# Layer 1 written out batch by batch, with the routing of layer 1's experts spread through it

## What is computed

```python
h    = layernorm(x)                      # rows of 256
g    = h @ Wr.T                          # 8 logits a row
top2 = the two largest of g, softmax over these two
y    = sum over the two experts e of  p_e * (silu(h @ Win[e].T) @ Wout[e].T)
x    = x + tanh(gate) * y
```

## Time and profile before

| | us |
|---|---|
| median of 3 runs (1465.41 to 1466.18) | 1465.86 |
| the profiled execution, its own time | 1465.79 |
| its span, first to last instruction | 1464.1 |
| PE busy (8832 matmuls) | 1292.1 (88%) |
| DVE busy | 1042.8 (71%) |
| ACT busy | 920.9 (63%) |
| POOL busy | 754.2 (52%) |

### The profile page before, as it was taken

One profiled execution on the slowest core, in us unless ns is written; L12 is line 12 of the kernel. 1 busy time (PEld: TensorE's weight loads), 2 busy tenths in 40 slices (PEclk: granted clock), 3 DMA queues, 4 the chain that ended last, 5 costly groups with the idle time before them and its releaser, 6 DMA issues. The chain is left out here.

```text
span 1464.1 us, 29786 instructions
## 1 busy us (share of the span) xinstructions
PE 1292.1 (88%) x8832; PEld 949.8 (65%) x8847; DVE 1042.8 (71%) x2336; ACT 920.9 (63%) x3577; POOL 754.2 (52%) x1068
## 2 busy tenths in 40 slices
PE   3899999999963899999999999999999994359991
PEld 2234444444432688888888888888888883349991
DVE  6466666666544888888888888888888877835554
ACT  1245454554534988888888888888888863313230
POOL 2355464645432566666666666666655542723331
PEclk8799999999985999999999999999999996569996
DMA  6443333323002311011110111101120005422225
GB/s 128 110 78 54 71 57 65 68 54 70 15 1 79 113 37 37 0 36 36 36 36 0 36 36 36 36 0 36 38 70 1 2 1 176 138 77 80 90 73 172
DMA packets 134339, 83.50 MB, mean 57 GB/s; under 512 B 67309, under 2 KB 129774, under 8 KB 134256
## 3 DMA queue, kind: packets, MB, share of 16 engines
q1 hardware_dynamic: 125280, 72.50, 19.4%
q0 software_dynamic: 3744, 8.43, 1.6%
q10 hardware_dynamic: 5232, 1.54, 0.5%
HBM read 50.01 MB, written 34.00 MB: 57 GB/s over the span
## 5 line engine op out<-in xcount | busy, mean ns | idle before, releaser
L1358 POOL TENSOR_TENSOR head_rstd<-head_rstd,minus_half 128x4 f32<-128x4 f32 x192 | 240.8, 1254 | 15.0
L1348 ACT ACTIVATE squares<-ps 128x128 bf16<-128x128 f32 x768 | 202.1, 282 | 49.9 <-PE ps L1320 39.7
L1320 PE MATMUL ps<-l_wb,xq 128*128 128x512 f16 (+1 forms) x1024 | 211.3, 329 | 6.7 <-DVE xq L1282 4.6
L1428 POOL TENSOR_TENSOR prob<-prob,rinv 128x512 f32<-128x512 f32 x128 | 135.5, 1058 | 118.0 <-DVE rinv L1423 116.5
L1415 ACT ACTIVATE prob<-ps,nmax 128x128 f32<-128x128 f32 x512 | 182.7, 384 | 11.4 <-DVE nmax L1408 11.4
L1378 ACT ACTIVATE headsT<-ps,l_hln 128x256 f32<-128x256 f32 (+1 forms) x256 | 166.6, 678 | 25.6 <-PE ps L1371 25.6
L1348 ACT ACTIVATION_READ_ACCUMULATOR squares<-ps 128x1 f32 x768 | 163.5, 214 | 0.0
L1364 DVE TENSOR_TENSOR heads_n<-ps,head_rstd 128x512 f32<-128x512 f32 x192 | 131.5, 685 | 38.8 <-POOL head_rstd L1358 38.8
L656 DVE TENSOR_REDUCE nmax<-ps 128x4 f32<-128x512 f32 x128 | 85.1, 682 | 75.4 <-PE ps L649 75.2
L1320 PEld LDWEIGHTS ps<-l_wb,xq 128*128 (+1 forms) x1024 | 101.0, 99 | 53.6 <-DVE xq L1282 5.0
L1401 PE MATMUL ps<-headsT 128*128 128x128 f32 x1024 | 135.2, 275 | 0.3 <-issue 0.3
(11 more groups left out here) (303 smaller groups left out, 2762.6 us busy)
## 6 DMA issues: line engine op xcount, KB each, us to landing
slots<-blank_slot SPq DMA_DIRECT2D x16, 1161.0 KB, 5.6
taken<-slots SPq DMA_DIRECT2D x23, 258.0 KB, 2.8
w_out_raw<-in_wprojT SPq DMA_DIRECT2D x8, 512.0 KB, 4.4
raw<-in_winT SPq DMA_DIRECT2D x4, 1024.0 KB, 9.2
raw<-in_woutT SPq DMA_DIRECT2D x4, 1024.0 KB, 6.1
back<-picked SPq DMA_DIRECT2D x8, 512.0 KB, 7.2
q_stack<-q_parts SPq DMA_DIRECT2D x48, 64.0 KB
k_blocks<-k_parts SPq DMA_DIRECT2D x192, 16.0 KB
```

The costliest lines, as they stand in the source:

```text
L1320: last = e.matmul(out, xq[:, k, which, slot_at], weights(k, hl, c0, n), start=(k == 0 and hl == 0), stop=(k == KD - 1 and hl == 1))
L1348: last = e.activation(squares[:, 4 * n + h, :], A[n][:, h * HD1:(h + 1) * HD1], ACT.Square, scale=HD1**-0.5, accum_out=hss[:, 4 * n + h:4 ...
L1358: e.tensor_tensor(hr[:, four], hr[:, four], t["half"][:, four], ALU.pow).then_inc(g_r[n].sem, 1)
L1428: e.tensor_tensor(prob[:, kind, :, :], prob[:, kind, :, :], spread(rinv[:, kind, :], P), ALU.mult).then_inc(g_p[kind].sem, 1)
```

## The change

1. All 16 batches of layer 1 are written out; there is no loop. The order strings get new words, and every step of the routing becomes a piece of them: `GS`, `GR`, `GN` (statistics, 1/sqrt, normalised rows), `GT` (two transposes into `S[0]`), `GU` and `GH` (ScalarE's copy of the turned rows, and of the high half), `GO` (number and low half of the packet), `GL` (two matmuls for the logits into `S[0]`), `GX` (copy of the logits), `GC:0` to `GC:2` (the choice for four batches, 16 chained instructions in three parts), `GK` (ranks, into `S[0]`), `GA` (addresses, 8 instructions), `GZ:0` to `GZ:3` (two scattering DMAs each). A batch's steps follow its attention by one to four batches.
2. `SC:0` waits in round 2 for `GU`, in round 3 for `GX`, and after a group also for the first instruction of `GA`.
3. The input weights of the experts go into `wb`, whose raw half takes the loads; they start when the last projection (`A`) is done, 4 of 8 pieces are split in the attention's block, 4 after it. SP waits for all scattered packets at the block's end.
4. WP_RING is 2 instead of 4. The blank table is written in the first four batches, 4 DMAs in each.
5. The block behind holds only the count, the table of tiles, and the splitting of the last 4 pieces. `back`, for the last sum, lies in `wb`.

```diff
-WP_RING = 4
+WP_RING = 2
 ORDER1 = {
-    "tensor": "A:0+ TQ:1 SC:0 PV:0- SC:1 O-- TQ:2+ PV:1- A:1+ PT:0 TQ:0+ A:2++ RT@0++ A:3 PT:1",
+    "tensor": "A:0+ TQ:1 SC:0 PV:0- SC:1 O-- TQ:2+ PV:1- A:1+ PT:0 TQ:0+ A:2++ RT@0++ GT@1-- GK@2--- GL@2-- A:3 PT:1",
-    "vector": "PT:1- SC:0 N:2+ RN@3+++ SC:1 RQ:4@2+ RS@3++++ RQ:3@1+ RQ:0@0+ R:0 RQ:1@0+ O-- QM:0- N:0+ R:1 QM:1- "
-              "PT:0 Q:0- Q:1- Q:2- N:1+ Q:3- Q:4- RQ:2@0+",
+    "vector": "PT:1- GX@3-- GA@3--- SC:0 N:2+ RN@3+++ GN@0-- SC:1 RQ:4@2+ RS@3++++ RQ:3@1+ RQ:0@0+ R:0 RQ:1@0+ O-- QM:0- N:0+ "
+              "R:1 QM:1- GS@2- GO@2-- PT:0 Q:0- Q:1- Q:2- N:1+ Q:3- Q:4- RQ:2@0+ GC:0@3-- GC:1@0--- GC:2@1---",
-    "scalar": "RA:0@0+ TQ:0 ST:2+ RE@1++ RA:3@3++ VE- RA:1@2++ RA:2@1++ TQ:1 ST:0+ SC:0 SC:1 CH@0+ TQ:2+ ST:1+",
+    "scalar": "RA:0@0+ TQ:0 ST:2+ RE@1++ GU@2-- RA:3@3++ VE- RA:1@2++ RA:2@1++ GH@1-- TQ:1 ST:0+ SC:0 SC:1 CH@0+ TQ:2+ ST:1+",
-    "gpsimd": "RS@2++++ R:1+ SU:1++ CO@3++ SU:2+++ SU:0+++ R:0++",
+    "gpsimd": "RS@2++++ R:1+ SU:1++ CO@3++ SU:2+++ SU:0+++ R:0++ GR@1- GZ:0@2--- GZ:1@3--- GZ:2@0---- GZ:3@1----",
-    "sync": "CL@0+ BL@1",
+    "sync": "CL@0+ BL:0@0 BL:1@1 BL:2@2 BL:3@3",
 }
...
+            if j == 2 and b >= 2:
+                e.wait_ge(a_gu.sem, a_gu.at(b - 2))
+            if j == 3 and b >= 2:
+                e.wait_ge(v_gx.sem, v_gx.at(b - 2))
+            if j == 3 and b >= 3 and (b - 3) % GROUP == GROUP - 1:
+                e.wait_ge(v_pos.sem, v_pos.at((b - 3) // GROUP))
...
+    EXPERTS_AFTER = {
+        "scalar": (("VE", LAST, B - 1, J - 1), ("GU", B - 2, J * B + 2), ("GU", B - 1, J * B + J + 2), ("GU", B - 1, J * B + J + 2)),
+        "vector": (("GS", B - 1, J * B + 2), ("GN", B - 1, J * B + J), ("GO", B - 1, J * B + J + 2), ("GC", B - 1, J * B + 2 * J + 1, 2)),
+    }
...
+    @s.piece("GX", "vector")
+    def _(e, b, i):
+        e.wait_ge(pe_gl.sem, pe_gl.at(b))
+        e.tensor_copy(logit[:, b % GROUP, :], S[0][:, 0:NE]).then_inc(v_gx.sem, 1)
...
+    @s.piece("GZ", "gpsimd")
+    def _(e, b, i, q):
+        if b % GROUP != GROUP - 1:
+            return
+        g, one = b // GROUP, b - GROUP + 1 + q
...
+        for which in range(2):
+            e.indirect_dma_start(
+                out=t["slots"][:, :], out_offset=bass.IndirectOffsetOnAxis(ap=at_u[:, g % 2, which, q:q + 1], axis=0),
+                in_=packet[:, one % PACKETS, :], in_offset=None, bounds_check=NE * SHELF - 1,
+                oob_is_err=False).then_inc(sent[g % 2], 16)
...
-        "sync": (("CL", 0, -4),) * 4 + (("CL", 1, 0),) * 4,
+        "sync": (("CL", 0, -4),) * 2 + (("CL", 1, 0),) * 6,
...
     with nc.Block() as block:
-        s.run(block, starting,
-              lambda owner, b: rounds(ORDER1[owner], b, False), lambda owner: part(owner, B - AHEAD, B + 1), (1, B - AHEAD))
+        s.run(block, starting, None, lambda owner: [], (0, 0))
```

More of the change, by code:

```diff
@@ new lines, in layer1_attention @@
+    wr, m_stats, m_mv, m_rstd, m_rows, u, packet = (t[n] for n in ("wr", "m_stats", "m_mv", "m_rstd", "m_rows", "u", "packet"))
+    logit, same, hide, number, first, second = (t[n] for n in ("logit", "same", "hide", "number", "first", "second"))
+    most, place, picks, before, tally, shelf = (t[n] for n in ("most", "place", "picks", "before", "tally", "shelf"))
+    pos, at, at_u, lower, all_b = (t[n] for n in ("pos", "at", "at_u", "lower", "all_b"))
+    wr_in, sets = nc.alloc_semaphore("wr_in"), nc.alloc_semaphore("route_sets")
@@ new lines, in _ @@
+    @s.piece("GK", "tensor")
+    def _(e, b, i):
+        if b % GROUP != GROUP - 1:
+            return
+        g = b // GROUP
+        e.wait_ge(v_pick.sem, v_pick.at(g))
+        e.wait_ge(v_PT[0].sem, v_PT[0].at(min(i, LAST)))
+        if b + 1 < B:
+            e.wait_ge(a_gu.sem, a_gu.at(b + 1))
+        e.wait_ge(v_gx.sem, v_gx.at(b))
+        here = S[0][:, 2 * GE:3 * GE]
+        e.matmul(here, lower[:, :], picks[:, :, :], start=True, stop=False)
+        e.matmul(here, all_b[:, :], tiled(before[:, :], GROUP), start=False, stop=False)
+        for j in range(GROUP - 1):
+            last = e.matmul(S[0][:, 2 * GE + (j + 1) * NE:3 * GE], all_b[:, :], tiled(picks[:, j, :], GROUP - 1 - j),
+                            start=False, stop=(j == GROUP - 2))
+        last.then_inc(pe_gk.sem, 1)
@@ L1737, in _ @@
-            e.wait_ge(s_makes, 6)
-            turn(0)
-            for g in range(NG):
-                route(g)
-                if g + 1 < NG:
-                    turn(g + 1)
-                rank(g)
-            e.wait_ge(s_count, 1)
-            e.matmul(bank[4][:, 0:NE], all_b[:, :], before[:, NG, :], start=True, stop=True).then_inc(s_count, 1)
+            e.matmul(bank[4][:, 0:NE], all_b[:, :], before[:, :], start=True, stop=True).then_inc(s_count, 1)
         @block.vector
         def _(e):
-            chain = Chain(nc, "c_route", 21 * NG + 13)
+            chain = Chain(nc, "c_route", 17)
```

435 lines of the change are left out of this document (235 added, 200 removed).

## The result

| | before | after |
|---|---|---|
| median, us (4 runs each, on one chip) | 1465.63 (1464.25 to 1466.18) | 1490.76 (1490.30 to 1492.20) |
| ratio, 95% interval | | 1.0175 [1.0157, 1.0192] |
| span of the profiled execution | 1464.1 | 1489.1 |
| first update of x in layer 1 | 506.04 | 522.99 |
| last update of x | 1216.15 | 1273.15 |

The change makes the kernel 25.1 us slower. The three stretches give the whole of it: the first update of x comes 17.0 us later, the 64 rounds from the first update to the last take 750.16 us instead of 710.11 (40.1 more), and from the end of the last update to the experts' first matmul it is 1324.60 - 1273.63 = 51.0 us instead of 82.0 (31.1 less). What follows is 0.9 us shorter. 17.0 + 40.1 - 31.1 - 0.9 = 25.1 us, the 25.0 of the spans.

What follows compares the result with a forecast made beforehand. TensorE, busy 100 of every 100 us, was taken to bound layer 1's attention. The terms -31.5 + 6.8 + 17 + 8 + 18 + 16 = +34.3 on 1465.8 gave 1500 us, range 1476 to 1530.

Steps and rivals of the forecast that it cites:

- writing out the loop: Layer 1's attention loop: writing it out costs or gains 0, since both forms of a batch take 45.64 us.
- behind the attention: From the last update of x to the experts' first matmul: 50.4 us against 82.0, 31.5 saved.
- TensorE's own work: In the attention: routing transposes and logit matmuls, 0.44 us in 14 batches, plus rank matmuls, 0.6: +6.8 us.
- `SC:0` waits for `GX`: In a batch's late round the score matmul waits for VectorE's logits copy, 1.2 us in 14 batches: +17 us.
- choice and addresses: On VectorE in the attention: 5.2 us for each of three groups, partly covered by waits: +8 us (0 to 16).
- scattering DMAs: Two a round between GpSimd's scalings make the next scaling late, 1.5 us in each of 12 rounds: +18 us.
- ring of two: At the start: projection weight loads come later, so ScalarE's splitting waits: +16 us (8 to 20).
- Rival A: Added work fits the queues' idle time; the attention pays only TensorE's 6.8 us and the start: 1453 us, chance 0.20.
- C: The start is not lost because the first rounds wait for other things anyway: 1488 us, sharing the forecast's chance.
- B: TensorE's wait for the logits copy gives VectorE and GpSimd time for choice and DMAs: 1478 us, chance 0.15.
- D: GpSimd becomes the bound in its twelve DMA rounds, 12 x 4 us instead of 18: 1530 us, chance 0.07.
- the 1510: Time in us if one scattering DMA of each pair met VectorE's rounding, each round costing about 2.3 us.

Runs made afterwards that it cites:

- n_unroll: The kernel before with its attention loop written out and nothing else: 1464.02 us, ratio 0.9998.
- c_gz1: The changed kernel with a group's eight scattering DMAs one a round over eight rounds, between GpSimd's second and third head sums: 1478.99 us, ratio 1.0099.
- a_ring4: The changed kernel with the ring of raw projection weights back at four and nothing else: 1472.65 us, ratio 1.0050.
- e_before2: The kernel before with the ring of raw projection weights cut from four to two and nothing else: 1481.14 us, ratio 1.0113.
- b_gx: The changed kernel with VectorE's logits copy (and shelf-base addition) ahead of its second copy of transposed probabilities: 1481.90 us, ratio 1.0119.
- j_gc: The changed kernel with the choice's 16 small operations in eight pairs at VectorE's waits, instead of three lots: 1487.02 us, ratio 1.0153.

## Why the prediction was right, and where not

| term | predicted | measured | by |
|---|---|---|---|
| writing out the loop | 0 | 0 | n_unroll |
| behind the attention | -31.5 | -31.1 | rows 3 to 5 and the trace after |
| TensorE's own work | +6.8 | +9.1 | 0.22 + 0.43 a batch, 14 batches |
| `SC:0` waits for `GX` | +17 | +12.0 | 0.86 a batch, 14 batches |
| choice and addresses | +8 | +5.1 | batches 5, 6, 9, 10, 13, less the plain ones |
| scattering DMAs | +18 | +12.5 | attention of c_gz1 |
| ring of two | +16 | +17.0 | first update; 18.1 and 16.7 by a_ring4 and e_before2 |
| batches 13 to 15 otherwise, and the experts | 0 | +0.5 | 1.4 - 0.9, not taken apart |
| sum | +34.3 | +25.1 | |

Choice and addresses are batch 5's 1.64 us over a plain one and 0.17 in batch 6 (read in c_gz1, where no DMA is in it), 1.64 and 0.18 in batches 9 and 10, and 1.45 in batch 13. The attention's four terms make 38.7 of its 40.1 us.

**The sign and the mechanisms** were right, each of them where it was put, but for one half of what the DMAs do (below): the ring, the wait for the logits, the drawn-out rounds with DMAs, and a tail of 50 us (predicted 50.4, measured 51.0). The two terms reckoned from a chain of durations, the tail and the ring, are within 1 us, and the chains came out link by link: to the first scattering DMA 17.5 us (16.2 predicted), the eight DMAs 10.0 (10.2), from there to the experts 23.4 (24.0); ScalarE's splits behind the late loads at 474.80 and 483.92 (474.9 and 484.1). The time came 9 us under the forecast, because three terms (the wait for the logits, the choice, the DMAs) were estimates between wide bounds, 43 us in all, and measured 29.6. TensorE's work, set 2.3 us too low, hid part of that, which is luck. The lower end of the range was not what the bounds add up to: they give 1461, not 1476 (the upper ends give 1530). Rival A is refuted: batches 2 to 14 average 48.2 us, over its 46.7, and the start cost all of 17 us. C is too, by a_ring4, though its 1488 is the number nearest to the measured one. B's time, 1478, would need DMAs and choice to be nearly free, and they cost 17.6. D did not come.

**TensorE's own work** was the term set furthest too low. "At most 0.22" for the logit matmuls came from their number of columns; they took 0.43 us (951.49 to 951.92 in b_gx). In the trace each of the two is two records, each as long as a transposition's one; columns did not make them shorter. The ranks' matmuls, 0.6 of this term in the prediction, are counted with the choice and addresses in the table, since nothing separates them there.

**The wait for the logits** was put at 1.2 us, 1.0 of it from the copy in between and the rest from VectorE's extra work. Together with the matmuls the prediction had 1.64 us a batch for routing, and the trace 1.51: the sum is right to 8%, its division less so. In its round `SC:0` stands 0.70 us further behind `TQ:1` than before, not 1.0, and b_gx shows that the copy in between is worth 0.60.

**The DMAs** were right in the first half of their mechanism and wrong in the second. The step was "the next scaling is 0.9 to 1.0 us late, or 1.3 more if a DMA meets VectorE". The late scaling did make TensorE wait, 1.36 us at 873.66, and by the rounds it made 6.9 of the 12.5 us; but in one round of the four of a group, not in all. No DMA in the loop was stretched (0.97 to 1.22 us, all of them). What happened in the other rounds is the reverse: the late scaling met VectorE's clamping, or the packet's low half, and held it, in the first group 1.50, 1.42 and 1.77 us in place of 0.42. Measured was 12.5 in place of 18, about 1.0 us for each of the twelve rounds that were reckoned with, but from nothing to 2.3 each; by c_gz1 it goes when the DMAs stand elsewhere, one a round.

The Trainium skill, page SBUF — State Buffer, section Who interferes with whom, says that GpSimd and a VectorE instruction in a two-port mode exclude each other, that a VectorE instruction with two inputs in SBUF and a GpSimd instruction that reads SBUF do too, and that whichever starts first keeps the ports for its whole duration. The traces agree with both directions: GpSimd's scaling, begun 0.21 us ahead, held an instruction of the choice in j_gc (0.19 to 1.03), and VectorE's low half, begun 0.16 us ahead, held GpSimd's addition (0.33 to 2.15). The low halves held GpSimd's DMAs too (0.97 to 1.89). The clampings at 832.29 and 844.43 began 0.12 and 0.05 us ahead of the scaling, while a DMA of GpSimd's ran, and were held all the same; by the page's rule that would need the DMA to have kept the ports, which no run shows. The prediction took only the second direction, and by it the 1510. It also said that the instruction beside the DMA of 2.71 us is not of the kinds the page lists; with two inputs in SBUF it is of the second kind, if a scattering DMA counts as an instruction that reads SBUF.

**The choice** was taken as the middle of 0 and 16 and came out at 5.1: two thirds of its 5.2 us a group cost nothing where it stood, and by j_gc pairs take 3.2 of what was left in batches 5, 9 and 13 (0.99, 1.04 and 1.13).
